# Inverse roots of the layer norms computed on GpSimd with a power operation, and the first norms of four units measured one a frame

## The reference

```python
def _layernorm(x, axis=-1, eps=1e-05):
    m = jnp.mean(x, axis=axis, keepdims=True)
    v = jnp.var(x, axis=axis, keepdims=True)
    return (x - m) / jnp.sqrt(v + eps)

x = x + jnp.tanh(g_xattn[0]) * attention(_layernorm(x), ctx, ctx, mask, Wq, bq, Wk, bk, Wv, bv, Wo, bo)
x = x + jnp.tanh(g_ffn[0]) * experts(_layernorm(x), Wg, W1, b1, W2, b2)   # top 2 of sigmoid(x @ Wg), tanh gelu
```

## Time and profile before

| what | value |
| --- | --- |
| median of 3 runs | 526.32 us (523.36 to 526.5) |
| profiled execution: its time, its span | 526.01 us, 524.3 us |
| TensorE, VectorE, ScalarE, GpSimd busy | 428.4, 332.1, 217.8, 171.4 us |
| frames with a softmax, in the trace | about 57 to 240 us |
| routing, in the trace | 240.4 to 274.8 us |
| expert stage, in the trace | 274.8 to 524.3 us |

### The profile page before, as it was taken

How to read it: one execution, slowest core, us unless ns; L and a number is a source line. 1 busy time by engine, 2 the same in 40 slices (tenths; PEclk the granted TensorE clock), 3 DMA queues, 4 the chain that set the end, 5 groups by cost and what they waited for, 6 DMA issues and landing times.

```text
span 524.3 us, 11190 instructions
## 1 busy us (share of the span) xinstructions
PE 428.4 (82%) x4040; PEld 326.2 (62%) x4040; DVE 332.1 (63%) x960; ACT 217.8 (42%) x549; POOL 171.4 (33%) x161
## 2 busy tenths in 40 slices
PE   5367767888888879897247999999999999999980
PEld 3234323555455544545226999999999999999970
DVE  5855687687886867668993555545554555555530
ACT  2130553455555654661004445444544454444420
POOL 8622601020112112111003354455445454554231
PEclk9855678899999997995557999999999999999995
DMA  7443332352535434341101133322322233233211
GB/s 208 103 139 105 81 116 67 90 157 90 152 109 145 128 97 131 115 122 41 46 1 53 32 46 50 53 43 43 55 50 44 43 54 52 42 45 51 33 21 20
DMA packets 35146, 40.26 MB, mean 77 GB/s; under 512 B 10431, under 2 KB 29747, under 8 KB 35091
## 3 DMA queue, kind: packets, MB, share of 16 engines
q0 software_dynamic: 12608, 27.48, 23.3%
q1 hardware_dynamic: 19953, 11.17, 7.6%
q10 hardware_dynamic: 2532, 0.89, 0.8%
HBM read 25.87 MB, written 9.50 MB: 67 GB/s over the span
## 4 chain that ended last, share of the span: by engine, by line
PE 60%; DVE 23%; DMA 6%; issue 4%; ACT 3%; POOL 1%; SPq 0%; ACTq 0%; DVEq 0%; POOLq 0%
PE bank L1218 7%; PE bank L1202 6%; PE bank L1204 6%; PE bank L1203 6%; PE bank L1220 6%; PE bank L1219 6%; PE bank L981 4%; DVE rowmax L666 4%; DMA W_stage<-in_L_ffn_W 3%; PE bank L1019 3%; PE bank L1128 3%; PE bank L998 3%; DVE W L729 2%; DVE stats L613 2%; PE bank L1166 2%
## 5 line engine op out<-in xcount | busy, mean ns | idle before, releaser
L1202 PE MATMUL bank<-xh,W 128*128 128x128 f16 x624 | 121.2, 220 | 1.0 <-DVE xl L896 1.0
L1203 PE MATMUL bank<-xl,W 128*128 128x128 f16 x624 | 121.1, 220 | 0.0
L1204 PE MATMUL bank<-xh,W 128*128 128x128 f16 x624 | 121.1, 220 | 0.0
L581 ACT ACTIVATE h<-bank,b1T 128x128 f32<-128x128 f32 x312 | 89.1, 370 | 70.1 <-PE bank L1204 68.2
L414 POOL DMA_INDIRECT out_rows<-y_sb,scatter_tab x39 | 63.8, 1635 | 113.5 <-DVE y_sb L913 107.4
L1218 PE MATMUL bank<-W,hh 128*128 x312 | 85.5, 274 | 0.0
L1220 PE MATMUL bank<-W,hl 128*128 x312 | 85.0, 273 | 0.0
L1219 PE MATMUL bank<-W,hh 128*128 x312 | 85.0, 273 | 0.0
L904 DVE CAST hh<-h 128x512 f16<-128x512 f32 x78 | 33.8, 434 | 75.9 <-ACT h L581 75.9
L666 DVE TENSOR_REDUCE rowmax<-bank 128x2 f32<-128x308 f32 x128 | 57.1, 475 | 26.1 <-PE bank L998 23.9
L525 ACT ACTIVATE probs<-bank 128x512 f32<-128x512 f32 x80 | 47.2, 595 | 47.9 <-PE bank L1076 36.7
(11 more groups left out here) (182 smaller groups left out, 683.7 us busy)
## 6 DMA issues: line engine op xcount, KB each, us to landing
W_stage<-in_L_ffn_W POOLq DMA_DIRECT2D x32, 512.0 KB, 4.1
xn_scratch<-attn SPq DMA_DIRECT2D x8, 256.0 KB, 2.2
qst<-qh SPq DMA_DIRECT2D x60, 32.0 KB, 2.4
X_late<-in_x SPq DMA_DIRECT2D x6, 256.0 KB, 4.9
out_rows<-X_late SPq DMA_DIRECT2D x6, 256.0 KB, 2.5
qst<-ql SPq DMA_DIRECT2D x28, 32.0 KB, 3.0
xg<-xn_scratch,gather_tab POOLq DMA_INDIRECT x39, 3.1
out_rows<-y_sb,scatter_tab POOLq DMA_INDIRECT x39, 3.9
```

The costliest lines, as they stand in the source:

```text
L581: ins = nc.scalar.activation(h32[s % 4][:, m * P:(m + 1) * P], H_BANKS[s % 4][:, m * P:(m + 1) * P], ACT.Gelu_apprx_tanh, scale=1.0 / W_SC ...
L1202: nc.tensor.matmul(dst, wh, xh[t % 3][:, cut], start=(c == 0), stop=False)
L1203: nc.tensor.matmul(dst, wh, xl[t % 3][:, cut], start=False, stop=False)
L1204: ins = nc.tensor.matmul(dst, wl, xh[t % 3][:, cut], start=False, stop=(c == KC - 1))
```

## The change

Two things. The inverse roots of all second norms, and of the first norms of units 4 to 7, are made on GpSimd by an addition of eps and a `pow` with -0.5 (`second_rstd`, `first_rstd`), and VectorE waits for them where it used to have them by its own Newton steps. The moments of units 4 to 7 for the first norm are taken one unit a frame, at item 2 of frames 0 to 3, in place of all four at item 5 of frame 0. The setup's inverse roots (units 0 to 3) stay as they were. On GpSimd, `first_rstd(u+4)` stands in front of the wait of the chunk of item 3, and `second_rstd(u-1)` in front of that of item 6 or 7; the last one stands behind the constants of the routing.

```diff
+            def second_rstd(v):
+                pool.wait_ge(moments_made, v + 1)
+                nc.gpsimd.tensor_scalar(var[:, :], mv[:, :, 1], EPS, None, ALU.add).then_inc(var_made, 1)
+                pool.wait_ge(var_made, v + 1)
+                nc.gpsimd.tensor_tensor(rstd[:, :], var[:, :], neg_half[:, :], ALU.pow).then_inc(rstd_made, 1)
+
+            def first_rstd(v):
+                pool.wait_ge(moments1_made, v - 3)
+                tiles = slice(2 * v, 2 * v + 2)
+                nc.gpsimd.tensor_scalar(var1[:, tiles], mv1[:, tiles, 1], EPS, None, ALU.add).then_inc(var1_made, 1)
+                pool.wait_ge(var1_made, v - 2)
+                nc.gpsimd.tensor_tensor(rstd1[:, tiles], var1[:, tiles], neg_half[:, :], ALU.pow).then_inc(rstd1_made, 1)
+
             for n, (_, high, low) in enumerate(chunks):
+                if n == SETUP_CHUNKS:
+                    pool.wait_ge(wT_made, 4)
+                    nc.gpsimd.memset(neg_half[:, :], -0.5).then_inc(var1_made, 1)
+                    pool.wait_ge(var1_made, 1)
+                if n >= SETUP_CHUNKS:
+                    u, i = w_steps[n - SETUP_CHUNKS]
+                    if i == W_SLOTS[u][1] and u + 4 < U:
+                        first_rstd(u + 4)
+                    if i == next(j for j in W_SLOTS[u] if j >= 6) and u >= 1:
+                        second_rstd(u - 1)
                 if n in bias_at:
...
             nc.gpsimd.iota(spare_row[:, :], pattern=[[0, 1]], base=N + 1, channel_multiplier=1, **exact).then_inc(consts2_made, 1)
+            second_rstd(U - 1)
...
             def layernorm1(v):
                 if v >= 1:
                     dve.wait_ge(q_filled, q_nth["q", v - 1])
+                if v >= 4:
+                    dve.wait_ge(rstd1_made, v - 3)
...
-                    if u == 0 and i == 5:
-                        first_norm(list(range(4, U)))
+                    if i == 2 and 4 <= u + 4 < U:
+                        v = u + 4
+                        dve.wait_ge(x_loaded[v], 16)
+                        row_moments([x_unit(v)], stats1[:, 2 * v:2 * v + 2, :], mv1[:, 2 * v:2 * v + 2, :]).then_inc(moments1_made, 1)
...
                         dve.wait_ge(q_free, q_nth["wo", v])
-                        row_moments([x_unit(v)], stats, mv, var, rstd, half_bits)
-                    if i == 6 and live(u - 1):
-                        refine_rstd(2, var, rstd, newton)
+                        row_moments([x_unit(v)], stats, mv).then_inc(moments_made, 1)
                     if i == 7 and live(u - 1):
                         v = u - 1
-                        refine_rstd(1, var, rstd, newton)
+                        dve.wait_ge(rstd_made, v + 1)
                         dve.wait_ge(a_filled, a_nth["attnT", v])
                         normalise(xn2, x_unit(v), mv, rstd).then_inc(ln2_done, 1)
```

More of the change, by code:

```diff
@@ L124, in build @@
             stats, mv = sb("stats", [P, 2, 6]), sb("mv", [P, 2, 2])
-            var, rstd, newton = sb("var", [P, 2]), sb("rstd", [P, 2]), sb("newton", [P, 2])
-            half_bits = sb("half_bits", [P, 2], I32)
+            var, rstd, neg_half = sb("var", [P, 2]), sb("rstd", [P, 2]), sb("neg_half", [P, 2])
             recip = sb("recip", [P, 2, N_HEADS])
@@ L189, in build @@
         ln1_done, x_biased = sem("ln1_done"), sem("x_biased")
+        moments1_made, var1_made, rstd1_made = sem("moments1_made"), sem("var1_made"), sem("rstd1_made")
+        moments_made, var_made, rstd_made = sem("moments_made"), sem("var_made"), sem("rstd_made")
         pv_evac = sem("pv_evac")
@@ L608, in _, with row_moments @@
             nc.vector.memset(ctxT[:, :, :, S:SP], 0.0)
-            def row_moments(src, stats, mv, var, rstd, half_bits):
+            def row_moments(src, stats, mv):
                 for j in range(2 * len(src)):
@@ L616, in row_moments, with guess_rstd @@
                     ins = nc.vector.bn_aggr(mv[:, j, :], stats[:, j, :])
-                step(ins)
+                return ins
+            def guess_rstd(mv, var, rstd, half_bits):
                 step(nc.vector.tensor_scalar(var[:, :], mv[:, :, 1], EPS, None, ALU.add))
@@ L650, in first_norm @@
                 tiles = slice(2 * units[0], 2 * units[-1] + 2)
-                row_moments([x_unit(u) for u in units], stats1[:, tiles, :], mv1[:, tiles, :], var1[:, tiles], rstd1[:, tiles], half_bits1[:, tiles])
+                step(row_moments([x_unit(u) for u in units], stats1[:, tiles, :], mv1[:, tiles, :]))
+                guess_rstd(mv1[:, tiles, :], var1[:, tiles], rstd1[:, tiles], half_bits1[:, tiles])
                 refine_rstd(3, var1[:, tiles], rstd1[:, tiles], newton1[:, tiles])
```

## The result

| what | before | after |
| --- | --- | --- |
| median of 4 runs each, on one chip | 525.46 us | 510.88 us (510.14 to 511.7) |
| ratio after to before | | 0.9704, interval 0.9662 to 0.9747 |
| profiled execution: its time, its span | 526.01, 524.3 us | 510.14, 508.3 us |

What follows compares the result with a forecast made beforehand. TensorE and VectorE were taken to bound the frames in turns, with VectorE's Newton work on the path. Terms by frame summed to 13.0 us, from 526.01 to 513.0 us, 513.3 us against the median; range 510 to 521 us.

Steps and rivals of the forecast that it cites:

- frame 5's term of 1.9 us: Frame 5: low half at item 7 moves forward by 0.7 (guess), then 1.4 together, then 0.6 more: 1.9 us.
- the limit of 1.8 us in frames 1 and 3: Frames 1 and 3: the next frame's load, ScalarE and TensorE's waits let about 1.8 us of 1.9 through.
- their terms: Forecast gains: frames 2 and 4 0.7 us each (the guess), frame 6 0.3 us, frame 8 1.4 us.
- rival A: GpSimd's power is slow and VectorE stands before the norm at item 7; gain nil at T = 3.9; chance 0.13.
- the cover: Time after the moments before the norm could start anyway: 2.2 us in frames 1, 3, 5 and 6, none in 8.
- T: Whole way over GpSimd from moments to norm (addition, power, three hand-overs): 1.0 us, between 0.5 and 2.0.
- Frame 0, 4.4 us: Frame 0 without `first_norm`: 3.56 us of TensorE idle time and 1.0 us of clock, against 0.15 us: 4.4 us.
- the 1.0 us for the full clock behind the stall: Frame 0: without the 3.56 us stall TensorE runs the following score and query at full rate, gaining 1.0 us.
- the next wait for VectorE, 1.26 us at 199.69 us: Frame 5: TensorE's following idle time behind VectorE, 1.26 us, was claimed to go too.
- rival C: Shorter idle times keep TensorE's clock up in frame 5 too: up to 2 to 3 us more, 510 us; chance 0.08.
- Frame 7, 0: Frame 7: of the same form as frame 6, where the other engines are the bound; gain 0.
- B: Frames 1 to 5: ScalarE, loads or TensorE's order late next, VectorE's time given back; 8.3 us, 518 us; chance 0.17.

Runs made afterwards that it cites:

- runs four and five: Changed kernel with two (four) or five (five) spare powers on GpSimd ahead of each second norm's own: 512.57 us and 532.92 us.
- the second one: Trace of the changed kernel run again without any edit: 508.32 us, ratio 0.9704.
- run one: Changed kernel, but first norms of units 4 to 7 together at item 5 of frame 0 with Newton steps, as before: 513.28 us, ratio 0.979.
- run six: Changed kernel, but the second norm of frame 5 (unit 4) keeps its thirteen Newton operations on VectorE: 514.08 us, one execution.
- run eight: Changed kernel with the first half of `find_places` before frame 8's norm, and the setup's inverse roots on GpSimd too: 510.66 us, ratio 0.9726.
- run two: Changed kernel, but the second norms' guess and Newton steps back on VectorE in every frame: 519.96 us, ratio 0.9903.

## Why the prediction was right or wrong

- **What failed.** Two steps of the sum: frame 5's term of 1.9 us, which put a wait as gone that stayed and put the clock at nothing (3.48 us measured, 2.31 of them busy time of TensorE), and the limit of 1.8 us in frames 1 and 3 (2.50 and 2.25 us measured). Together they are 2.7 of the 3.4 us by which the pieces exceed the sum. Both are taken up below.
- **The mechanism and most terms were right.** The VectorE work of items 5 to 7 and `first_norm` were on the path, the way over GpSimd is covered in frames 1 to 5 and paid in frame 8, no stage gave the time back. In frames 6 and 7 VectorE waits for it too (1.15 us), but there the others are the bound, as forecast: with 2.46 us piece 6 is only 0.2 us longer. Pieces 2, 4, 6 and 8 came out within 0.15 us of their terms (0.83, 0.83, 0.24 and 1.35 us), and rival A's break-even of 3.9 us is near the 3.7 that runs four and five give. That one is in part luck: the cover was 1.95 us and not 2.2, the loss 10.6 us for each us of T and not 8, and against these two stands a gain that was larger than the forecast's.
- **T = 1.0 us measured 1.14 us,** within its bounds; the power's 0.5 was too small by 0.2, the hand-overs too large by 0.1. It cost 0.14 us at most, in frame 8.
- **Frame 0, 4.4 us, was right in sum.** The 3.56 us of waiting turned into 3.90 us less idle time. The 1.0 us for the full clock behind the stall was not seen as such, and that the sum fits is luck: busy time fell by 0.54 us in this trace and 1.55 us in the second one. The query behind the stall went from 2.71 to 1.89 us as forecast, but the low clock at the start of the piece lasted 2.9 us longer. And run one, with the stall still there, has the full clock behind it, so the stall isn't shown to be what lowered it.
- **Frames 1 and 3, 1.8 us each, measured 2.50 and 2.25 us.** The failed step is "these allow about 1.8 us", the limit by the load and ScalarE. The low half moved forward and ScalarE's wait for the load, 1.49 us, vanished wholly, as argued; the waits of TensorE for maxima fell by 2.16 us in piece 1, and 0.37 us of its busy time went too, at an unchanged clock of 1.00. Of the waits I had counted 0.9, 0.44 and 0.46 of the 0.74; I had left out that the one of item 6, 0.99 us (the like of the earlier trace rows, which I used for frames 2 and 4 only), stands in the odd frames too. It fell to 0.16 us. Gone are 2.90 us, new are 0.78, net 2.13. Where the 0.37 us come from isn't settled (with two more powers, run four, they are back in both pieces, also at a clock of 1.00).
- **Frame 5, 1.9 us, measured 3.48 us.** The term was 1.9 us of waiting, with "the next wait for VectorE, 1.26 us at 199.69 us" gone. Idle time fell by 1.17 us only (0.81 by run six), for that wait is 1.37 us in the kernel after; it stands behind the low half's maxima in both. The other failed step is the clock, nothing in the sum and a rival C with a chance of 0.08. The row that spoke for it was on the table: a score took 0.44 us in place of 0.30. The windows of before show its size, a granted clock of 0.51 from 198 to 204 us. Run six gives 2.40 us of busy time for it, inside the "up to 2 to 3 us" of rival C. So the trace before already held it; whether it would go was uncertain (run eight), and why the clock falls in this piece stays open.
- **Frame 7, 0, measured 0.47 us,** but the piece lies between 16.88 and 17.47 us over ten of the eleven traces of changed kernels (all but the one with five more powers), with 16.89 us in run two, which has the Newton steps there. It isn't a gain that the change can claim.
- **The difference in all:** 0.70 + 0.45 in pieces 1 and 3, 1.58 in piece 5, 0.47 in piece 7 and 0.2 in the other five make 3.4 us more than the sum of 13.0. Less 0.5 us for the longer expert stage, and 0.1 more in the setup, this gives the 16.0 us between the spans; the medians lie 14.6 us apart, because the profiled execution lies 0.55 us above its median before and 0.74 us below it after.
- **B did not happen:** what is late next in the odd frames (ScalarE's 0.78 us, TensorE's own order) comes after nearly all of the saving.
- **The first call.** The Trainium skill, GPSIMD Engine Reference, Instruction dispatch, has about 6 us for the first call of a freshly loaded function. The first power of the changed kernel took 0.73 us (68.55 us), as all others; the trace doesn't show such a cost.

## What to carry to other kernels

Cut both traces at the same instructions and split each piece into TensorE's busy and idle time: the idle part shows which waits an edit removed (to some 0.9 us in piece 0 here), the busy part is for the most part the clock, which in one stage was here larger than the waits. When small serial operations stand on a full engine's path, two instructions on an idle engine can take them over if their way (here 1.14 us) is shorter than the work that stands between producer and consumer anyway (here 1.95 us). Within that cover the power's speed hardly matters; beyond it, it does (a way of 2.46 us cost 1.3 us in the uncovered frame 8 and over 0.6 us in each odd one, a way of 4.42 us more than the whole gain). When GpSimd hands something to VectorE, look at what GpSimd starts next: a long instruction there can hold a short one of VectorE.

## What the runs showed of the hardware

- GpSimd's power on 128x2 elements takes 0.72 us, on 128x6 1.36 us: an estimate from these two sizes is 0.16 us for each element a partition and 0.40 us fixed. An addition on 128x2 takes 0.22 us.
- A norm of 0.73 us on VectorE took 2.78 us next to a GpSimd affine select of 2.52 us: its first instruction, started 0.12 us before the select, took 0.41 us, its second, started 0.2 us behind the select's start, 2.45 us. Beside the issue of a load and a memset of 1.82 us the norm took 2.86 us.
- TensorE's granted clock fell to 0.50 for some us in piece 5 in all three kernels with Newton steps there, in both with added powers and in run eight, which has neither; in six others it stayed at 1.00. Behind a stall of 3.56 us it was 0.50, behind one of 2.97 us 1.00. Over twelve traces, piece 0 with the same 142 records of TensorE had 24.1 to 27.5 us of busy time. A difference below 3 us in such a stage says nothing of an edit unless a wait shows it too.
